# Moving the normalisation, the x statistics, the additions and the norm matmul to other places within a chunk

## What is computed

```python
def spatial_descriptor(x, k):      # k = 5
    corrs = [sum over channels of x * x shifted by (di, dj) for di in range(k) for dj in range(k)]
    return stack(corrs, axis=1)    # 25 maps

g = gn(x)                          # group norm, 32 groups of 16 channels
gs = spatial_descriptor(g, 5)
gs = gs / sqrt(sum(gs * gs, axis=1, keepdims=True) + 1e-6)
feat = concatenate([g, gs], axis=1)
y = x + relu(einsum('bchw,oc->bohw', feat, W) + bias[None, :, None, None])
```

## Time and profile before

| | us |
|---|---|
| median of 3 runs (4456.75 to 4460.8) | 4460.77 |
| the profiled execution | 4458.1 |
| its span in the trace | 4456.4 |
| PE busy in the span | 3936.7 (88%) |
| DVE busy | 3559.3 (80%) |
| ACT busy | 1898.3 (43%) |
| POOL busy | 2281.9 (51%) |
| first layer's chunks, from the first to the last pick matmul | 62.7 to 2594.6 |
| second layer | about 2700 to 4456 |

### The profile page before, as it was taken

One profiled execution on the slowest core, in us unless ns is written; L12 is line 12 of the kernel. 1 busy time (PEld: TensorE's weight loads), 2 busy tenths in 40 slices (PEclk: granted clock), 3 DMA queues, 4 the chain that ended last, 5 costly groups with the idle time before them and its releaser, 6 DMA issues. The chain is left out here.

```text
span 4456.4 us, 76765 instructions
## 1 busy us (share of the span) xinstructions
PE 3936.7 (88%) x23656; PEld 2172.9 (49%) x23657; DVE 3559.3 (80%) x3528; ACT 1898.3 (43%) x2964; POOL 2281.9 (51%) x1793
## 2 busy tenths in 40 slices
PE   5999999999999999999999965789888888888885
PEld 3556555555555655656556642334333333333332
DVE  6887788787888788878878766689866799999993
ACT  3444444444444544444444513444333333333332
POOL 3555555555555555555555514355544444556442
PEclk9999999999999999999999977889998999999897
DMA  4444344544544444444443334444456566565551
GB/s 183 154 170 176 132 173 167 176 148 157 188 155 162 168 151 167 177 147 158 176 167 138 121 80 171 191 184 189 188 219 237 194 235 250 224 245 208 226 211 50
DMA packets 252266, 781.57 MB, mean 175 GB/s; under 512 B 98151, under 2 KB 98151, under 8 KB 229991
## 3 DMA queue, kind: packets, MB, share of 16 engines
q1 hardware_dynamic: 219600, 417.85, 26.8%
q0 software_dynamic: 32288, 358.95, 20.8%
HBM read 428.22 MB, written 409.08 MB: 188 GB/s over the span
## 5 line engine op out<-in xcount | busy, mean ns | idle before, releaser
L1062 DVE TENSOR_TENSOR arena<-arena 128x2048 f32<-128x2048 f32 (+5 forms) x539 | 1442.5, 2695 | 263.0 <-ACT arena L675 223.8
L1402 PE MATMUL psum<-arena 128*128 128x512 f32 x1072 | 606.7, 650 | 295.5 <-ACT arena L695 209.4
L1208 PE MATMUL psum<-arena 128*128 128x256 f16 (+1 forms) x6344 | 763.1, 276 | 47.2 <-DVE arena L808 34.4
L447 POOL TENSOR_TENSOR arena<-arena 128x512 f16<-128x512 f32 x512 | 721.5, 1417 | 146.5 <-ACT arena L597 140.6
L1231 PE MATMUL psum<-arena 128*128 128x512 f16 x2048 | 776.8, 379 | 0.0
L1233 PE MATMUL psum<-arena 128*128 128x512 f16 x2048 | 776.2, 379 | 0.0
L1232 PE MATMUL psum<-arena 128*128 128x512 f16 x2048 | 776.2, 379 | 0.0
L1208 PEld LDWEIGHTS psum<-arena 128*128 128x128 f16 x6344 | 610.9, 102 | 160.1 <-DVE arena L808 44.5
L673 ACT ACTIVATE arena<-arena 128x4096 f32 x67 | 242.5, 3619 | 1045.5 <-issue 1045.5
L456 POOL TENSOR_TENSOR arena<-arena 128x512 f32 (+1 forms) x512 | 635.1, 1273 | 10.7 <-ACT arena L611 6.7
L820 DVE BATCH_NORM_STATS2 bny<-arena 128x6 f32 (+1 forms) x512 | 355.6, 694 | 341.2 <-POOL arena L456 328.0
(11 more groups left out here) (161 smaller groups left out, 4328.5 us busy)
## 6 DMA issues: line engine op xcount, KB each, us to landing
arena<-in_x SPq DMA_DIRECT2D x64, 2048.0 KB, 13.3
wide_planes<-arena SPq DMA_DIRECT2D x128, 1024.0 KB, 5.3
y_planes<-arena SPq DMA_DIRECT2D x64, 2048.0 KB, 7.8
arena<-arena SPq DMA_DIRECT2D x1536, 8.0 KB, 1.8
arena<-wide_planes,arena POOLq DMA_INDIRECT x72
arena<-plane_records,arena POOLq DMA_INDIRECT x67
arena<-y_planes,arena POOLq DMA_INDIRECT x67
out<-arena POOLq DMA_INDIRECT x67, 7.9
```

The lines of the kernel that those rows point to most:

```text
L447: pool.tensor_tensor(gl[:, ct, slot], g32[:, ct % 2, :], gh[:, ct, slot], ALU.subtract).then_inc(s_gl, 1)
L1062: ins = dve.tensor_tensor(dst, a, b, ALU.max)
L1208: return pe.matmul(dst, w, m, start=(k == 0), stop=(k == nk - 1))
L1402: pe.matmul(dst, diag[:, s, 0, :], bufs[:, u, b * CW:(b + 1) * CW], start=True, stop=False)
```

## The change

It reorders each chunk on four engines; SyncE is untouched.

- ScalarE: `normalise` of chunk c + 3 goes to the start of the chunk: channel tiles 0 and 1 ahead of the square, tile 2 between square and root, tile 3 behind `after`. Chunk 5, where c + 3 is the first chunk of the next image, keeps nearly the old order.
- GpSimd: low parts 0 to 2 first, then additions 0 and 1, then `fh` and `fl` (now `halves`), then additions 2 and 3, then low part 3.
- VectorE: `x_stats` goes from the end of the chunk to its start, ahead of the masks (only chunk 7's statistics stay at the end of chunk 3); the descriptor comes behind the second mask, `y_stats` 0 behind the third, the others behind the fourth. Two small copies in `wide_rows` become a maximum of a slice with itself.
- TensorE: `norm` goes from behind the first gram block to behind `tail`.

```diff
@@ -438,42 +438,49 @@
 
         @block.gpsimd
         def _(pool):
-            def low_parts(i, c):
+            def low_parts(i, c, cts=range(CT)):
 
                 n0 = (i * CH + c) * CT
                 slot = slice((c % RING) * CW, (c % RING + 1) * CW)
-                for ct in range(CT):
+                for ct in cts:
                     pool.wait_ge(s_gh, n0 + ct + 1)
                     pool.tensor_tensor(gl[:, ct, slot], g32[:, ct % 2, :], gh[:, ct, slot],
                                        ALU.subtract).then_inc(s_gl, 1)
 
-            def residual(i, c):
+            def residual(i, c, outs=range(CT)):
 
                 n0 = (i * CH + c) * CT
-                for o in range(CT):
+                for o in outs:
                     y = xs(o, c * CW, CW, i % 2)
                     pool.wait_ge(s_relu, n0 + o + 1)
                     pool.tensor_tensor(y, y, relu[:, o % 2, :], ALU.add).then_inc(s_added, 1)
 
+            def halves(i, c):
+
+                n = i * CH + c
+                half = c % 2
+                pool.wait_ge(s_fn, n + 1)
+                if not (isinstance(i, int) and i == 0 and c < 2):
+                    pool.wait_ge(grouped[half], (i * (CH // 2) + c // 2) * GROUPED)
+                pool.sem_inc(s_issue, 1)
+                pool.tensor_copy(fh[:, half, :], fn).then_inc(s_th, 1)
+                pool.wait_ge(s_th, n + 1)
+                pool.tensor_tensor(fl[:, half, :], fn, fh[:, half, :], ALU.subtract).then_inc(s_t, 1)
+
             def image(i, first, last):
                 for c in range(CH):
-                    n = i * CH + c
-                    half = c % 2
-                    pool.wait_ge(s_fn, n + 1)
-                    if not (isinstance(i, int) and i == 0 and c < 2):
-                        pool.wait_ge(grouped[half], (i * (CH // 2) + c // 2) * GROUPED)
-                    pool.sem_inc(s_issue, 1)
-                    pool.tensor_copy(fh[:, half, :], fn).then_inc(s_th, 1)
-                    pool.wait_ge(s_th, n + 1)
-                    pool.tensor_tensor(fl[:, half, :], fn, fh[:, half, :], ALU.subtract).then_inc(s_t, 1)
-                    if c > 0:
-                        residual(i, c - 1)
-                    elif not first:
-                        residual(i - 1, CH - 1)
-                    if c + 3 < CH:
-                        low_parts(i, c + 3)
-                    elif not last:
-                        low_parts(i + 1, c + 3 - CH)
+                    ahead = (i, c + 3) if c + 3 < CH else None if last else (i + 1, c + 3 - CH)
+                    soon = ahead and c + 3 != CH
+                    back = (i, c - 1) if c else None if first else (i - 1, CH - 1)
+                    if soon:
+                        low_parts(*ahead, cts=(0, 1, 2))
+                    if back:
+                        residual(*back, outs=(0, 1))
+                    halves(i, c)
+                    if back:
+                        residual(*back, outs=(2, 3))
+                    if ahead:
+                        low_parts(*ahead, cts=(3,) if soon else range(CT))
 
             for c in range(3):
                 low_parts(0, c)
@@ -580,14 +587,15 @@
                 act.wait_ge(s_gavg, 2 * k + 2)
                 act.activation(grs[:, :], psum[:, BANK_N, CT:2 * CT], ACT.Sqrt, bias=epsg[:, :]).then_inc(s_gsq, 1)
 
-            def normalise(i, c, first=False, between=None):
+            def normalise(i, c, cts=range(CT), first=False):
 
                 n0 = (i * CH + c) * CT
-                act.wait_ge(s_newton, 3 * i + 3)
-                if not first:
-
-                    act.wait_ge(s_chunk_used, i * CH + c - RING + 1)
-                for ct in range(CT):
+                if 0 in cts:
+                    act.wait_ge(s_newton, 3 * i + 3)
+                    if not first:
+
+                        act.wait_ge(s_chunk_used, i * CH + c - RING + 1)
+                for ct in cts:
                     if not (isinstance(n0, int) and n0 + ct < 2):
                         act.wait_ge(s_gl, n0 + ct - 1)
                     act.sem_inc(s_carry_a, 1)
@@ -596,8 +604,6 @@
                                    scale=grstd[:, ct:ct + 1])
                     act.activation(gh[:, ct, (c % RING) * CW:(c % RING + 1) * CW], piece, ACT.Identity,
                                    bias=gbias[:, ct:ct + 1], scale=grstd[:, ct:ct + 1]).then_inc(s_gh, 1)
-                    if between and ct == 1:
-                        between()
 
             def conv_out(chunk, o):
                 n = chunk * CT + o
@@ -621,25 +627,28 @@
                 for c in range(CH):
                     n = i * CH + c
                     first = isinstance(n, int) and n == 0
+
+                    ahead = (i, c + 3) if c + 3 < CH else None if last else (i + 1, c + 3 - CH)
+                    soon = ahead and c + 3 != CH
+                    if soon:
+                        normalise(*ahead, cts=(0, 1), first=first)
                     act.wait_ge(s_pick, n + 1)
                     act.activation(sq, psum[:, BANK_A, 0:QW], ACT.Square).then_inc(s_sq, 1)
+                    if soon:
+                        normalise(*ahead, cts=(2,))
                     act.wait_ge(s_norm, n + 1)
                     act.activation(sq, psum[:, BANK_N, 0:QW], ACT.Sqrt, bias=epsd[:, :]).then_inc(s_root, 1)
                     if not first:
                         for o in range(CT):
                             conv_out(n - 1, o)
+                    if ahead and not soon:
+                        normalise(*ahead, cts=(0, 1))
                     if c + 1 < CH:
-                        turn = lambda: after(i, c + 1)
+                        after(i, c + 1)
                     elif not last:
-                        turn = lambda: after(i + 1, 0)
-                    else:
-                        turn = lambda: None
-                    if c + 3 < CH:
-                        normalise(i, c + 3, first=first, between=turn)
-                    elif not last:
-                        normalise(i + 1, c + 3 - CH, between=turn)
-                    else:
-                        turn()
+                        after(i + 1, 0)
+                    if ahead:
+                        normalise(*ahead, cts=(3,) if soon else (2, 3))
                     if c == STATS_AT and not last:
                         group_root(i + 1)
 
@@ -828,7 +837,8 @@
                 dve.wait_ge(s_added, (n + 1) * CT)
                 dve.tensor_tensor(pairs_m[:, :, :, 1:half], y[:, :, :, 1:W - 2:2], y[:, :, :, 2:W - 1:2], ALU.max)\
                     .then_inc(s_pairs, 1)
-                dve.tensor_copy(pairs_m[:, :, :, 0:half + 1:half], y[:, :, :, 0:W:W - 1]).then_inc(s_pairs, 1)
+                dve.tensor_tensor(pairs_m[:, :, :, 0:half + 1:half], y[:, :, :, 0:W:W - 1], y[:, :, :, 0:W:W - 1],
+                                  ALU.max).then_inc(s_pairs, 1)
                 dve.wait_ge(s_pairs, n * 4 + 2)
                 if not (isinstance(n, int) and n == 0):
                     dve.wait_ge(wide_stored, n * 16)
@@ -837,7 +847,8 @@
                 dve.wait_ge(s_middle, n + 1)
                 dve.tensor_tensor(wide[:, :, :, 1:W - 2:2], wide[:, :, :, 0:W - 3:2], y[:, :, :, 3:W:2], ALU.max)\
                     .then_inc(s_pairs, 1)
-                dve.tensor_copy(wide[:, :, :, W - 1:W], wide[:, :, :, W - 2:W - 1]).then_inc(s_pairs, 1)
+                dve.tensor_tensor(wide[:, :, :, W - 1:W], wide[:, :, :, W - 2:W - 1], wide[:, :, :, W - 2:W - 1],
+                                  ALU.max).then_inc(s_pairs, 1)
                 dve.wait_ge(s_pairs, n * 4 + 4)
                 dve.tensor_tensor(wide[:, :, :, 2:W:2], wide[:, :, :, 2:W:2], y[:, :, :, 0:W - 3:2], ALU.max)\
                     .then_inc(s_wide, 1)
@@ -869,7 +880,14 @@
                         res = []
                     else:
                         res = [lambda o=o: y_stats(i - 1, CH - 1, o) for o in range(CT)]
-                    between = [[lambda: descriptor(i, c)], res[0:1], res[1:2], res[2:4]]
+                    between = [[], [lambda: descriptor(i, c)], res[0:1], res[1:4]]
+                    if c == 0 and first:
+                        for e in range(3):
+                            x_stats(1, e)
+                    if c < 4 and left >= 1:
+                        x_stats(i + 1, c + 3)
+                    elif c > 4 and left >= 2:
+                        x_stats(i + 2, c - 5)
                     if c + 1 < CH:
                         masks_of(i, c + 1, between)
                     elif not last:
@@ -884,15 +902,8 @@
                         wide_rows(i, c - 1)
                     elif not first:
                         wide_rows(i - 1, CH - 1)
-                    if c == 0 and first:
-                        for e in range(3):
-                            x_stats(1, e)
-                    if c < 4 and left >= 1:
-                        x_stats(i + 1, c + 3)
-                        if c == 3:
```

(8 more changed lines are left out.)

## The result

The changed kernel takes 4980.65 us (median; 4975.68 to 4980.96) against 4458.76 us: a ratio of 1.117, interval 1.116 to 1.118. It is 522 us slower. The sign and the mechanism came as forecast; the size did not: 4860 us was forecast, and 4981 lies above the range's upper end of 4960. The second layer is as it was. The whole difference lies in the first layer's chunks, which now run from 63.0 to 3116.5 us, where they ran from 62.7 to 2594.6. One of the four executions of experiment 5 fell in a slower state (6763 us, granted clock 0.56) and is left out of its median.

The account below looks back on a forecast made before the run. TensorE bounds the first layer at 18.9 us a chunk. Profiled 4458.1 us, less 77 gained by the looser order, plus 478 for 42 stalls on late loads, gives 4859, forecast as 4860 us; range 4780 to 4960.

Parts of the forecast that it names:

- the floor: First layer: TensorE's own work over 127 chunk intervals takes 2387.5 us, against 2531.1 us in the trace.
- the load is not late enough: Rival, chance 0.05: the quarter of x lands before the statistics need it, they cost nothing, 4384 us.
- the 42 waits with the clock after them: Chunks 1, 5, 7: TensorE idle while statistics wait for x, then slow clock; 34.1 us an image, 478 us.
- the turn of the loop, made longer: Idle in chunk 0's picks as the loop turns: forecast to stay at 2.1 to 2.5 us, nothing added.
- the kernel without either: The new order without late loads: 4458.1 us less 77 us gained, plus 2.7, 4384 us.
- (b): Loop's turn: 2.1 to 2.5 us idle in the middle of chunk 0's picks, released only by issue; forecast to stay.
- The gain without the waits: First layer: excess over TensorE's least time falls from 144 to 66 us without the late loads, 77 us gained.
- (c): Chunks 0 to 4: some 1 us lost because VectorE's round of about 19 us equals TensorE's; forecast to go.
- VectorE's round did get looser: Each chunk: row maxima fall from 8.1 to some 6 to 7 us, so VectorE no longer holds TensorE.
- The stalls cost more: Rival, 0.10 above 4960: clock stays low through grams and convolutions, or transfers exceed 16 us; 126 more, 4986 us.
- `fh` isn't delayed: Rival, 0.12 for 4686 to 4780: GpSimd's `fh` at its old time, each stall 4.15 us shorter, 4686 us.

Follow-up runs that it names:

- experiment 5: The kernel before with only the x statistics moved to the start of the chunk, all other orders kept: 4769.5 us.
- experiments 1: The changed kernel with the statistics of chunks 1, 5 and 7 back at the end of the chunk: 4502.7 us.
- experiment 2: The changed kernel with SyncE's loads of chunks 4, 6 and 0 issued ahead of the regrouping: 4413.95 us, ratio 0.989.
- experiment 4: The changed kernel with SyncE waiting in chunk 0 for the picks before it issues the store of row maxima: 4940.15 us.
- experiment 6: The kernel before with x statistics at the chunk's start and loads ahead of the regrouping, other engines' orders kept: 4459.65 us, ratio 1.000.
- experiment 7: The changed kernel with loads ahead of the regrouping and, in chunk 4, the group norm's spreads ahead of the row maxima: 4375.2 us, ratio 0.981.

## Why the prediction came out as it did

**Right.** That TensorE bounds the chunks at 18.9 us; that the floor leaves at most 144 us to gain; that the load of chunks 4, 6 and 0 stands behind `fh` in SyncE's queue; that the statistics of chunks 5, 7 and 1 would wait for it, 42 times, in front of all masks. All 42 are in the trace, in those chunks, and experiments 1, 2 and 5 show the chain link by link. The rival "the load is not late enough" would have been 4384 us; with the load moved (experiment 2) the kernel gives 4414.

**Wrong: three terms of the sum, all too small.** 4981 - 4860 = 121 us, and three runs split it (to about 4 us, as the kernel before differs by that much between them):

| term | predicted | measured | from |
|---|---|---|---|
| the 42 waits with the clock after them | 478 | 526 | 4940.15 - 4413.95 (experiments 4 and 2) |
| the turn of the loop, made longer | 0 | 41 | 4980.65 - 4940.15 (experiment 4) |
| the kernel without either | 4384 | 4414 | experiment 2 |

The three differences are 48 + 41 + 30 = 119 us. The other 2 are rounding in the prediction: 4859 + 2.7 is 4862, and it said 4860. The waits are within the bounds given for them. What had no bound was the turn, and the gain of 46 lies below the 50 to 100 allowed; these two carried the time out of the range.

*The waits, 12.5 us each and not 11.4.* The idle was 10.6 us on average (10.8 in chunk 1, 9.3 in chunk 5, 11.6 in chunk 7), where I had 10.4, 8.5 and 10.4. For chunk 7 I took chunk 6 as 18.9 us long, and rows 3 show 18.1: 0.8 us of idle was lost in the sum there. In chunk 6 `fh` came at T = 9.4, not 9.05, and the twelve transfers took 8.43 us, not 7.57, so the load went out at 19.65, not 18.45. A landing of 12.85 us, a little under the 13.2 I took, gave some of it back. Why the transfers took longer to issue stays open. The slow clock cost 2.2 us: behind the 42 waits 24 matmuls take 5.03 us on average (4.39 to 5.30) and 2.79 undisturbed. I took 1.6 from the pair of rows 4 and 5. That row stood behind a gap of 2.44 us; I had seen that a gap of 10 us might cost up to 2.4 and still summed with 1.6. Idle and clock make 12.8 us; the term of 12.5 is a difference against experiment 2, whose chunks 5 and 6 are themselves 12 us longer in all than undisturbed ones.

*The turn of the loop.* "(b) stays" was the step that failed, and no part of the sum covered it. It said that the turn's idle stays at 2.4 us, without asking what sets it, and the idle became 4.3. Chunk 7 became 14 us longer, but VectorE's work in it did not, so the row maxima ended ahead of the chunk's end and their 1 MB store went out ahead of the turn, not behind it as before. I had costed each engine's moves inside a chunk, and not what a stretched chunk does to the phase of the next transfer.

*The gain without the waits, 46 us and not 77.* By the traces experiment 2 stands 95 us above the floor, where the sum had 66. Chunk 0 holds 51 of them, where I had 38 (34 for 14 turns, of which there are 13, and 4 for the first chunk): I had priced the turn's idle and not the clock behind it, which falls in 10 of 13 turns (24 matmuls in 4.46 us), and in the kernel before in 6. So a part of (c), which I put down to VectorE's long round, was that clock, and stayed: chunk 0 still lasts 21.2 or 22.9 us, by whether the clock falls. The other part, 8 us in chunks 1 to 3, went as said. Chunks 5 and 6 hold 12 that I had at nothing, 7 of them the clock behind the wait for the spreads. Chunk 4 holds 31, where I had 28. VectorE's round did get looser, as said, and more than said: the maxima take 5.8 us, and the small maximum 0.28 us, since low part 3 does not meet it.

**The rivals.** "The stalls cost more" named the clock staying low through the convolutions; it does not (1.00 from 1416.2 to 1426.9 behind the long gap, 5 us after work resumes). The time ended on that rival's side of the range by other terms. "`fh` isn't delayed" is what experiment 5 made, 4769.5 us: its 304 us for the stalls fit (4769.5 - 4460.5 = 309), and the 77 us of gain that it also counted need the orders that experiment 5 leaves out.

## What to carry to other kernels

When a consumer is moved forward in an engine's order, ask of every wait at its head when its producer arrives, and follow that producer back through its own queue: here VectorE's statistics, a load, twelve transfers, GpSimd's cast, ScalarE's relus. A move on one engine can delay a transfer on a queue that the diff does not touch; moving that transfer too turned 1.117 into 0.989, and taking one more wait off the chunk's end gave 0.981. A gap on TensorE is to be costed with the clock after it, from the row with the gap nearest in length, and what lies at a fixed place such as a loop's turn is to be checked again once chunks change length.

## What the runs showed of the hardware

A gap of 2.1 to 2.5 us at the turn (1.8 to 2.9 in the experiments) was enough for the lower clock in some images and not in others, mostly at a cost of about 1.7 us: behind 6 of 13 turns in the kernel before, 10 in experiment 2, 5 in experiment 4, 13 in experiment 6 and 4 in experiment 7. The length of the gap doesn't decide it: in the kernel before, 2.17 us was followed by it in image 14 (chunk 0 lasts 22.7 us) and not in image 13 (21.2 us). What does stays open. Differences between orders of up to some 15 us (an estimate, 9 turns at 1.7 us) can be this alone. A bulk store of 1 MB, issued 1.6 us ahead of the turn of TensorE's loop, lengthened the idle there from 2.4 to 4.3 us. A load of 2 MB landed in 8.0 to 8.9 us after issue with no store of y beside it, and in 12.5 to 14.7 us with one. Small instructions of VectorE wait for a whole GpSimd instruction: 1.22 us against 0.27 us alone for a maximum with two inputs from the same memory, 1.17 against 0.22 us for a copy, both of 64 elements.
